# Moving the issue of a small DMA behind an exponential, and spreading the first routing, in a fused attention and expert kernel

## What is computed

```python
x = x + tanh(g_xattn) * attention(layernorm(x), ctx)
x = x + tanh(g_ffn) * experts(layernorm(x))
# attention: 16 heads of 8 features; softmax over q.k of the same tokens and, apart from it,
#   over q.ka of the context; out = h_main*(1-gate) + h_aux*gate; then Wo
# experts: sigmoid(x @ gate_w.T) + bias -> best 4 of 8 groups -> best 8 experts per token,
#   weights normalised and scaled by 2.5;
#   y = sum over experts of w[e] * (silu(x @ Wg[e]) * (x @ Wu[e])) @ Wd[e], plus one shared expert
```

## Time and profile before

| | |
|---|---|
| time, median of 3 runs | 897.53 us (895.03 to 897.87) |
| the profiled execution | 898.08 us, of which its span 896.3 us |
| TensorE busy, share of the span | 849.5 us, 95% |
| VectorE, ScalarE, GpSimd | 76%, 63%, 72% |
| attention stage | 0 to about 319 us |
| mean granted TensorE clock | 0.988 of full speed |

### The profile page before, as it was taken

One profiled execution on the slowest core, in us unless ns is written; L12 is line 12 of the kernel. 1 busy time (PEld: TensorE's weight loads), 2 busy tenths in 40 slices (PEclk: granted clock), 3 DMA queues, 4 the chain that ended last, 5 costly groups with the idle time before them and its releaser, 6 DMA issues.

```text
span 896.3 us, 20102 instructions
## 1 busy us (share of the span) xinstructions
PE 849.5 (95%) x6765; PEld 660.1 (74%) x6765; DVE 683.8 (76%) x1652; ACT 562.4 (63%) x963; POOL 644.2 (72%) x605
## 2 busy tenths in 40 slices
PE   5899999989997899999999999999999999999997
PEld 3466666666665577888888888887888888888885
DVE  6888888878887747867867966976877776786665
ACT  4477778768776556557557557556656656655554
POOL 2567878877874247778777877787788777787775
PEclk9999999999999889999999999999999999999999
DMA  5577677686672055554654755654554645554652
GB/s 133 171 181 178 176 191 178 179 192 161 163 189 51 20 130 128 132 141 108 162 131 107 176 126 127 143 147 109 145 143 118 163 121 133 132 140 125 139 141 60
DMA packets 113619, 125.24 MB, mean 140 GB/s; under 512 B 27936, under 2 KB 75936, under 8 KB 112080
## 3 DMA queue, kind: packets, MB, share of 16 engines
q1 hardware_dynamic: 110640, 123.43, 55.2%
q10 hardware_dynamic: 2880, 0.59, 0.4%
HBM read 103.52 MB, written 19.96 MB: 138 GB/s over the span
## 4 chain that ended last, share of the span: by engine, by line
PE 78%; ACT 6%; DVE 4%; DMA 4%; issue 4%; POOL 1%; SPq 1%; ACTq 1%; POOLq 0%; DVEq 0%
PE bank L1918 19%; PE bank L1920 19%; PE bank L1919 19%; PE bank L1300 5%; PE bank L1287 4%; PE bank L1274 2%; ACT prob L787 2%; PE bank L1244 1%; DMA stack_k<-k_scratch 1%; PE bank L1321 1%; PE bank L1308 1%; DMA k_scratch<-parts_k 1%; ACTq L781 1%; POOL hid L1621 1%; PE bank L1250 1%
## 5 line engine op out<-in xcount | busy, mean ns | idle before, releaser
L1621 POOL TENSOR_TENSOR hid<-act,cwb 128x512 f32<-128x512 f32 x264 | 430.1, 1638 | 139.1 <-DVE act L1836 93.2
L1836 DVE TENSOR_TENSOR act<-silu,bank 128x512 f32<-128x512 f32 x264 | 180.2, 683 | 142.0 <-ACT silu L1670 134.7
L1670 ACT ACTIVATE silu<-bank 128x512 f32<-128x512 f32 x264 | 157.5, 597 | 208.6 <-PE bank L1920 208.2
L1918 PE MATMUL bank<-xhi,weights_hi 128*128 128x512 f32 x528 | 210.2, 398 | 0.0
L1920 PE MATMUL bank<-xlo,weights_hi 128*128 128x512 f32 x528 | 207.7, 393 | 0.0
L1919 PE MATMUL bank<-xhi,weights_lo 128*128 128x512 f32 x528 | 207.4, 393 | 0.0
L1840 DVE TENSOR_TENSOR hlo<-hid,hhi 128x512 fp32r<-128x512 f32 x264 | 199.7, 757 | 1.5 <-ACT hhi L1675 1.4
L985 DVE TENSOR_REDUCE mx<-bank 128x4 f32<-128x512 f32 x256 | 167.7, 686 | 30.0 <-PE bank L1274 24.1
L787 ACT ACTIVATE prob<-bank 128x1024 f32<-128x1024 f32 x128 | 130.9, 1022 | 77.9 <-PE bank L1287 76.2
L1675 ACT ACTIVATE hhi<-hid 128x512 fp32r<-128x512 f32 x264 | 164.7, 624 | 6.1 <-POOL hid L1621 5.5
L1920 PEld LDWEIGHTS bank<-xlo,weights_hi 128*128 128x128 f32 x528 | 99.3, 188 | 22.4
(11 more groups left out here) (227 smaller groups left out, 1009.5 us busy)
## 6 DMA issues: line engine op xcount, KB each, us to landing
cwb<-wts_scratch SPq DMA_DIRECT2D x176, 384.0 KB, 5.4
stack_k<-k_scratch SPq DMA_DIRECT2D x30, 384.0 KB
k_scratch<-parts_k SPq DMA_DIRECT2D x15, 384.0 KB, 3.4
stack_q<-q_scratch SPq DMA_DIRECT2D x30, 192.0 KB
k_scratch<-parts_k SPq DMA_DIRECT2D x15, 256.0 KB, 4.2
q_scratch<-parts_q SPq DMA_DIRECT2D x15, 192.0 KB, 2.4
xin<-in_x_dram SPq DMA_DIRECT2D x16, 128.0 KB, 2.3
cin<-in_ctx_dram SPq DMA_DIRECT2D x16, 128.0 KB, 2.6
```

The source lines that it names most:

```text
L1621: pool.tensor_tensor(h_buf[k][:], a_buf[k][:], cwb[slot][:, q % GP, :], ALU.mult).then_inc(h_ok, 1)
L1670: act.activation(s_buf[k % RS][:], g_bank[k % 2][:], ACT.Silu).then_inc(s_ok, 1)
L1836: nc.vector.tensor_tensor(a_buf[k % RS][:], s_buf[k % RS][:], u_bank[k % 3][:], ALU.mult).then_inc(a_ok, 1)
L1918: nc.tensor.matmul(bank, w[0], mh, start=first, stop=False)
```

## The change

On ScalarE, the issue of the shift rows of batch b + 1 moves from behind the first exponential of batch b (and its copies) to right behind the second one. The copy of V moves from round 1 to round 3 of the even batch, in the last body too (where it was at the odd batch). On TensorE and VectorE, the maxima of the last four batches (28 to 31) are turned one round later and copied out at u = 2. The first group's preparation is laid out anew over the last body: the norm at rounds 2 and 3 of batch 28, transposes and operand copies in batch 29, logits and exponentials at the end of batch 29 (in bank `misc[1]` instead of `misc[0]`), `first_lo` at the start of batch 30, and the routing over batches 30 and 31 with its reciprocal in four pieces instead of one; its weights are turned a round later. `minus_max` and `turn_max` of batch 31 now wait for the exponentials, since these read the same bank. Two weight conversions change places. SP waits until the first pair of `cwb` transfers has landed before it issues the second pair.

```diff
@@ attention: lists @@
-                + [(n, c, r) for n in range(LIGHT, NC - 1) for c in range(CH) for r in (0, 3)]
-                + [(NC - 1, 0, 1), (NC - 1, 0, 2), (NC - 1, 1, 0)])
+                + [(LIGHT, c, r) for c in range(CH) for r in (0, 3)]
+                + [(NC - 2, 0, 0), (NC - 2, 1, 0), (NC - 2, 1, 3), (NC - 1, 0, 1), (NC - 1, 0, 2), (NC - 1, 0, 3), (NC - 1, 1, 0)])
-    ROUTE_AT = {(2, 1): (0,), (2, 3): (1, 2), (2, 4): (3, 4, 5), (2, 5): (6, 7), (2, 6): (8, 9), (2, 7): (10, 11), (3, 0): (12, 13)}
+    ROUTE_AT = {(2, 1): (0, 1 / 4), (2, 2): (2 / 4,), (2, 3): (3 / 4, 1), (2, 4): (2, 3), (2, 5): (4, 5), (2, 6): (6, 7),
+                (2, 7): (8, 9), (3, 0): (10,), (3, 1): (11, 12), (3, 2): (13,)}
@@ SP @@
         for gr in range(2):
+            if gr == 1:
+                sp.wait_ge(cw_in[0], 32)
@@ ScalarE, body @@
                     exps(b, r)
+                    if r == 1 and not (last and k == BODY - 1):
+                        shift_rows(b + 1)
                     if r == 0 and not first:
                         copy_o(b - 1, 1 - odd)
...
-                    if r == 0 and not (last and k == BODY - 1):
-                        shift_rows(b + 1)
-                    if last and k == 0:
-                        if r < 2:
-                            first_norm(r)
-                        if r == 3:
-                            first_operand()
-                            first_xT()
-                    if last and k == 1 and r == 1:
-                        first_exp()
...
-                    if (odd, r) == ((1, 3) if last else (0, 1)) and more:
+                    if (odd, r) == (0, 3) and more:
...
-                    if last and k == 3 and r == 2:
+                    if last and k == 0 and r >= 2:
+                        first_norm(r - 2)
+                    if last and k == 1 and r == 1:
+                        first_operand()
+                    if last and k == 1 and r == 2:
+                        first_xT()
+                    if last and k == 1 and r == 3:
+                        first_exp()
+                    if last and k == 3 and r == 3:
                         first_wT()
@@ VectorE @@
+            if 0 < part < 1:
                 dve.wait_ge(fs_ok, 1)
-                nc.vector.reciprocal(sig, sig).then_inc(fs_ok, 1)
+                cols = slice(int(4 * part - 1) * E, int(4 * part) * E)
+                nc.vector.reciprocal(sig[:, cols], sig[:, cols]).then_inc(fs_ok, 1)
...
                     if u == UNITS - AHEAD - 1 and one_more:
+                        if b == NB - 2:
+                            dve.wait_ge(fe_ok, 1)
                         minus_max(b + 1, 1 - odd, min(n + 3 + odd, NC))
-                    if u == 1 and one_more:
+                    if u == (2 if last or (left == 1 and k == 3) else 1) and one_more:
                         evac_nmax(b + 1)
...
-                    if last and k == 0 and u == 7:
+                    if last and k == 2 and u == 0:
                         first_lo()
@@ TensorE, body @@
+                late = last or (before_last and k == BODY - 1)
...
+                    if r == 1 and late and one_more:
+                        wait(pe, nm_ev, b + 1)
+                        if b == NB - 2:
+                            pe.wait_ge(fe_ok, 1)
+                        turn_max(b + 1)
...
-                    if (odd, r) == ((1, 2) if last else (0, 0)) and more:
+                    if (odd, r) == (0, 0) and more:
...
-                    if r == 0 and one_more:
+                    if r == 0 and one_more and not late:
                         wait(pe, nm_ev, b + 1)
                         turn_max(b + 1)
...
-                    if last and k == 0 and r == 2:
+                    if last and k == 1 and r == 0:
                         first_turn_x()
-                    if last and k == 1 and r == 0:
+                    if last and k == 1 and r == 3:
                         first_logits()
-                    if last and k == 3 and r == 1:
+                    if last and k == 3 and r == 2:
                         first_turn_w()
```

More of the change, by code:

```diff
@@ L831, in first_exp @@
             act.wait_ge(flg_mm, 1)
-            act.activation(f_sig[:].rearrange("p k e -> p (k e)"), misc[0][:, 0:K * E], ACT.Exp,
+            act.activation(f_sig[:].rearrange("p k e -> p (k e)"), misc[1][:, 0:K * E], ACT.Exp,
                            scale=-1.0).then_inc(fe_ok, 1)
@@ L1057, in first_route @@
                 nc.vector.tensor_scalar(sig, f_sig[:].rearrange("p k e -> p (k e)"), 1.0, None, ALU.add).then_inc(fs_ok, 1)
+            if 0 < part < 1:
                 dve.wait_ge(fs_ok, 1)
-                nc.vector.reciprocal(sig, sig).then_inc(fs_ok, 1)
+                cols = slice(int(4 * part - 1) * E, int(4 * part) * E)
+                nc.vector.reciprocal(sig[:, cols], sig[:, cols]).then_inc(fs_ok, 1)
             if part == 1:
-                dve.wait_ge(fs_ok, 2)
+                dve.wait_ge(fs_ok, 4)
+                nc.vector.reciprocal(sig[:, 3 * E:], sig[:, 3 * E:]).then_inc(fs_ok, 1)
+                dve.wait_ge(fs_ok, 5)
                 logit = sig.rearrange("p (k g h e) -> p k g h e", k=K, g=NG, h=2)
@@ L1334, in first_turn_x @@
         def first_turn_x():
-            pe.wait_ge(fg_ev, 1)
+            pe.wait_ge(v_ev, NC)
             pe.wait_ge(fxn_ok, 2)
@@ L1342, in first_logits @@
             pe.wait_ge(fxT_ok, 1)
-            pe.wait_ge(flo_ok, 1)
+            wait(pe, nm_ev, NB - 1)
             for k in range(K):
-                ins = nc.tensor.matmul(misc[0][:, k * E:(k + 1) * E], f_xT[:, k * P:(k + 1) * P], gwT[:],
+                ins = nc.tensor.matmul(misc[1][:, k * E:(k + 1) * E], f_xT[:, k * P:(k + 1) * P], gwT[:],
                                        start=True, stop=True)
@@ L1349, in first_turn_w @@
         def first_turn_w():
-            pe.wait_ge(v_ev, NC)
+            pe.wait_ge(flo_ok, 1)
             pe.wait_ge(frw_ok, 1)
@@ L1431, in body @@
                         project_qk(n + 3, 1 - i)
-                    if (odd, r) == ((1, 2) if last else (0, 0)) and more:
+                    if (odd, r) == (0, 0) and more:
                         if last:
-                            pe.wait_ge(fe_ok, 1)
-                        else:
-                            wait(pe, ka_ev, min(n + 3, NC))
+                            pe.wait_ge(fg_ev, 1)
+                        wait(pe, ka_ev, min(n + 3, NC))
                         project_v(n + 1, (i + 1) % 2, 0)
                         project_v(n + 1, (i + 1) % 2, 1)
-                    if r == 0 and one_more:
+                    if r == 0 and one_more and not late:
                         wait(pe, nm_ev, b + 1)
```

## The result

| | before | after |
|---|---|---|
| median, on one chip | 896.63 us (7 runs) | 891.83 us (7 runs, 887.52 to 893.98) |
| ratio after / before | | 0.994 (0.9913 to 0.9966) |
| the profiled execution (its span) | 898.08 (896.3) | 889.23 (887.4) |
| mean granted TensorE clock | 0.988 | 0.992 |

The account below looks back on a forecast made before the run. TensorE carries the attention path, with small repeating waits for late exponentials. Terms 0 + 13.2 - 5.3 + 0.4 + 1.5, another -0.8, gave +9.0 on 898.08: 906.5 us against the median; range 892 to 918, likeliest case 899 to 918.

Parts of the forecast that it names:

- Part 1: ScalarE and TensorE, issue moved behind the second exponential: even batches gain 0.39, odd ones lose 0.33 to 0.43; sum about 0.
- at 3.2: Odd batches: shift rows issued 3.2 us after the first exponential instead of 1.90, behind both halves of the stack_k load.
- part 2: DMA queues: odd batches' rows land behind the stack_k load and TensorE waits, 0.94 us over 14 loads, +13.2 us.
- +0.33 to +0.43: Odd batches: TensorE's matmul after the round comes this many us later, as ScalarE issues ahead of the Q and K copies.
- The even batch's -0.39: Even batches: the second exponential starts at 141.97 instead of 142.36, so TensorE's 0.38 us wait goes.
- Chunks at 16.4 or less: Sign that the forecast is wrong: a chunk of two batches takes 16.4 us or less, against 16.74 before.
- at most 2.02 + 0.8: SP's queue: latest issue of stack_k's second half after an odd batch's first exponential, in us, ahead of the rows.
- Rival B: Rows pass the stack_k load, or the load moves ahead by itself; 893.3 us, chance 0.27.
- Part 3: Last four batches: TensorE's wait for the turned maxima and half-clock time behind it go, -5.3 us; later effects +0.4 and +1.5.
- The last wait and the experts' start: End of attention: TensorE waits longer for turn_att, +0.4; the experts' first hid comes later, +1.5 (0 to 3) us.
- SP's wait: Experts' start: waiting for the first cwb pair before issuing the second gives back about 1 us at the first hid.
- against it: 191.03: Evidence against the rows passing the load: rows issued 0.95 after it released TensorE at 191.03, 8.58 after the load's issue.

Follow-up runs that it names:

- the held issue: The changed kernel, with ScalarE waiting until the second exponential has finished before it issues the shift rows; 900.63 against 895.64 us, ratio 1.0054.
- the rows alone: The kernel before, with only the shift rows issued behind the second exponential and the V copy in the fourth round; 890.51 against 895.64 us, ratio 0.9954.
- two issues: The changed kernel, with the shift rows' DMA issued a second time by ScalarE, into a spare tensor; 890.17 against 895.57 us, ratio 0.9957.

## Why the prediction was wrong

- **Part 1, ScalarE: wrong, and this is the step that failed.** "Behind it ScalarE now has the issue (0.62 and about 0.1 to the next start) ahead of the copies of Q and K": I put the issue in series behind the exponential. It runs beside it, from 0.01 after its start. The misreading came from the earlier trace rows: the issue at 149.88 falls together with the end of the weight conversion, and I took the one for the cause of the other. The row beside it, which I hadn't read, is VectorE's copy of the turned maxima, in the kernel before in the even and the odd batch:

```profile
141.39 0.22 DVE L1002 COPY nmaxT<-bank 64x128 bf16<-64x128 bf16 x1
...
149.64 0.22 DVE L1002 COPY nmaxT<-bank 64x128 bf16<-64x128 bf16 x1
```

  It ends at 141.61 and 149.86, the issues follow at 141.63 and 149.88. It isn't chance: each of the 31 issues inside the loop of batches follows this copy by 0.02 or 0.03, in even and odd batches. So the issue waited for its data, and only the exponential behind it waited for the queue. In the changed kernel the data is there 0.37 ahead (the copy ends at 147.59) and nothing is left of the wait. All that followed hangs on this: the issue "at 3.2" of part 2 came at 2.24. "+0.33 to +0.43" in odd batches was right for an issue that waits (0.41 with the held issue) and 0 for this one. The even batch's -0.39 was right (-0.40). "Chunks at 16.4 or less" was my own sign of being wrong, and a chunk is 16.34.
- **The odd batch's gain, which I hadn't asked for.** With the issue free, the odd batch should have gained 0.4 as well; it does, up to the third exponential (4.00 instead of 4.39 after the first). Then ScalarE waits for nshift. Before, nshift was just ahead of its use; this cover is gone. Batches 1, 3 and 25 have no such limit, and there the fourth exponential came 0.4 sooner: the first two took 8.00 and 8.16 for 8.40, while 25 lost it again to a row wait (8.93 for 8.40). Forecast for part 1: 0; measured -4.8 in the twelve even batches that were undisturbed before.
- **Part 2, +13.2: the mechanism right in the main, its condition not met.** Rows behind both halves of stack_k were late in 29 of 43 batches, by up to 2.21 us: among them batch 27 of the change and nine with the held issue; and all but one wait were gone with the second half 1 us behind the rows. The condition was the issue at 3.2, against a second half "at most 2.02 + 0.8". (The 2.02 was no upper end: in the same profile the load is at 2.24 and 2.56 in batches 9 and 5.) At 2.24 the rows stand between the halves or ahead of both (stack_k's issue is mostly at 1.6 to 2.6, its second half 0.8 later), and three waits of 0.47 to 0.95 came even there. Rival B names "the load is issued later than 3.2"; the true threshold is lower for the same reason. With the held issue, the kernel that I had in mind, the rows cost 10.0 us of waits (13.2 forecast, 3.7 in the change), and the time was 0.5% above the kernel before, where my sum says 1.0%: the sign was right for that kernel, the size about half. The rule of the Trainium skill ("DMA: Bandwidth & Descriptors", Queues, rings and completion order), by which the engines take turns between queues, gave the right time for another reason: by it the held issue's ten late rows wouldn't exist.
- **Part 3, the turned maxima: right.** -5.3 forecast, -5.25 in batch 29 and -0.44 in batch 30 measured. Batch 28, which I had left out, gained as well in most executions: 8.2 to 8.3 in eight of the eleven profiles with the new order, 9.51 and 9.66 in the two before; in the change's own profile it stayed at 9.51, behind the wait of 1.79. How much of batch 29's gain is clock isn't fixed: with the rows alone, 2.66 of it came without the tail's change. What I missed is the other end of the late turn, batch 27: I named the queue mechanism in part 2 and didn't ask it of the one odd batch whose issue really moves to 3.2. It cost 1.99 in this execution.
- **The last wait and the experts' start: right.** +0.4 and +1.5 forecast, +2.2 measured; the last wait is for att, 3.11 (about 3 forecast). For SP's wait I had about 1; the profiles show about 0.5 at the first hid, and at the end nothing that can be told.
- **The chances.** B had 0.27, and "against it: 191.03" spoke of rows issued behind the load, which says nothing on where the new issue would stand. Its 893.3 lies 1.5 from the median; it counted part 1 at 0 (was -5) and left out batch 27 (+2) and the start and the scatter of row waits. That it came so near is in part luck.

## What to carry to other kernels

Before adding an instruction's duration to a chain, find out which row ended the wait ahead of it: an issue that starts when an activation ends may have waited for its data at that moment. Behind the start of the longest operation of an engine a DMA issue costs only what sticks out; and when a queue's order decides a landing, look where every late issue stands against every large load, batch by batch, the exceptions first. A gain of one engine ends at the next producer in line, here a value of GpSimd that had been just in time.

## What the runs showed of the hardware

- **A DMA issue of ScalarE runs beside the activation ahead of it**: 0.62 us, started 0.01 after a 1.02 us exponential, with the next activation 0.92 behind the exponential's start as without an issue. Behind an issue that ends later, the next activation starts 0.10 to 0.11 after its end: 150.50 to 150.61 before, 142.11 to 142.21 with the held issue, 149.42 to 149.52 with two issues.
- **A small DMA behind a large load of another queue often came out with that load.** The 16 KB on ScalarE's queue, issued behind both 384 KB halves on SP's, were late in 29 of 43 cases (in batch 27 their packets passed 4.2 to 5.7 us after the issue, with the load's last); between the halves in 27 of 125; ahead of both in 0 of 28. What share the order has and what the distance in time isn't separated.
- **The clock behind a wait isn't a function of the wait's length.** Waits of TensorE of 2.27 were followed by 0.50 (1.2 GHz) twice and by 1.00 (2.4 GHz) once. At the start of batch 28, a wait of 1.79 was followed by 0.62, but one of 2.21, in the kernel without SP's wait, by 1.00:

```profile
269.53 0.23 PE L1294 MATMUL bank<-stack_q,stack_k 64*128 64x128 bf16 x1 [2.21 <-DMA stack_q<-nmaxT]
...
270.00:274.00 4.00, 4.00 (x74) 3.07 (x69) 3.62 (x10) 2.95 (x4) 1.00 (x2) 1.00 0.02 4
```

  What decides it stays open.
